# Indirect scatters on GpSimd tied to other engines' progress: the first sorting scatters after the twentieth follow VectorE, three of four result scatters per tile follow TensorE

## The chip, the cores and the metric

The kernel runs on one core of one Trainium2 chip. The metric is the device time of one execution in microseconds (us). Before the change three runs took 594.9, 598.07 and 599.07 us, median 598.07.

## The reference

What is computed is one block on x of 32 sequences of 256 tokens, 128 wide (8192 tokens). A layer norm is followed by two branches that are added to x: a gated linear recurrence ("the mixer": projection, causal convolution with 4 taps, a scan along the sequence, gates, output projection), and a mixture of 8 experts of which each token uses 2. Cut to what matters:

```python
x = L0_attn_x
xn = _layernorm(x, axis=-1)
x = x + _L0_attn_ref(xn, ...) + _L0_ffn_ref(xn, ...)

# mixer, per token and channel
_, h = jax.lax.associative_scan(_linrec_combine, (alpha_c, gated), axis=1)
y = h * C_gate + D * x_conv
out = jnp.einsum('blh,...', y * jax.nn.silu(z), W_out)

# experts
logits = xt @ w_gate
top_logits, sel = jax.lax.top_k(logits, TOP_K)          # TOP_K = 2
probs = jax.nn.softmax(top_logits, axis=-1)
h = silu(xt @ w1[e]) * (xt @ w3[e]);  y = h @ w2[e]
out = sum over the two chosen e of y * probs
```

## The kernel before, in words

The program is written by hand: each engine has its own list of instructions, and semaphores alone order them across engines. An instruction that is done adds one to its semaphore; a DMA adds 16 when it has landed. `wait_ge(s, n)` holds the engine's queue until semaphore s has reached n.

Stages:

- **Preparation.** x is loaded, normalised and transposed; TensorE makes the router's logits; VectorE chooses two experts for each token (`choose`) and counts a slot for each token and choice (`place(0)` for the first quarter of the tokens, `place(1)` for the rest). Then VectorE builds small tables (which expert each tile of sorted rows has, and where its rows begin): 38 short operations, most made with `link`, which adds one to `s_dve` and then waits for that same increment before it lets VectorE go on.
- **Sorting scatters.** GpSimd writes each token's normalised row to its two slots in a DRAM buffer `moe_in`: 64 groups of 128 tokens by 2 choices, so 128 indirect DMAs of 128 rows of 532 bytes, numbered i = 0 to 127 (line 540). The first 32 need `place(0)` alone. The function `ahead(i)` makes those from i = 49 on wait for `s_ch`, which counts VectorE's seven chain operations in each mixer step.
- **Mixer, steps 0 to 11.** Each step g takes 512 tokens. VectorE's part of a step is the convolution taps (`tap`, which counts `s_cv` after the second tap-pair of a kind and `s_taps` after the last), the chain of seven (`chain`, `s_ch`) and `softplus` (`s_dt`). Before these, ScalarE copies TensorE's projection out of PSUM, for which it waits on TensorE's `s_xr` and `s_xp`.
- **Experts.** 36 tiles of 512 sorted rows (the last has 256; four of them are split between two experts). SyncE loads each tile's rows and weights. TensorE's queue in one cycle is: first products of tile k (`up`: two halves, which count `s_h1` and `s_h3`), transposes of the rows of tile k + 1 (`transp`, `s_T`), second products of tile k - 1 (`down`, `s_y`). Between them ScalarE rounds (`xhi`, `whi`) and applies silu, and VectorE forms the low parts (`xlo`, `wlo`), the product of the halves (L1422) and the scaled result (`scale_y`, L1483, which counts `s_yc`) in a ring of 8 buffers. GpSimd then scatters the tile's result to `moe_out` in four indirect DMAs of 128 rows of 512 bytes (line 548): 142 in all. In the queue of before, all four of a tile wait only for `s_yc` and `s_dst` of that tile.
- **Mixer, steps 12 to 16, and the sums.** When all scatters have landed, GpSimd issues 16 accumulating DMAs (line 562) that add the experts' results; SyncE stores what is complete.

The order of the work is the order of each engine's list; no planner or scheduler is in it.

Of the kernel before, what the change touches and what calls it, by code (L numbers as in the profile page):

```python
# [22 lines left out]
EXPERTS, HID, TOP_K = 8, 256, 2  # L23
# [5 lines left out]
MOE_TILES = FULL + MIXED + 1  # L29
# [11 lines left out]
STEPS_A = 12  # L41
# [13 lines left out]
STORES = (5, 6)  # L55
OUTS = 8
CHAIN = 7


def block_kernel(nc, x, W_in, conv_w, conv_b, W_x, W_dt, b_dt, A_log, D_skip, W_out,  # L60
# [5 lines left out]
    with ctx:  # L66
# [6 lines left out]
        def sem(name):  # L73
            return ctx.enter_context(nc.semaphore(name))
# [140 lines left out]
        s_dve = sem("s_dve")  # L215
# [24 lines left out]
        s_taps = sem("s_taps")  # L240
        s_cv = sem("s_cv")
# [7 lines left out]
        s_dt = sem("s_dt")  # L249
# [3 lines left out]
        s_ch = sem("s_ch")  # L253
# [14 lines left out]
        s_T = sem("s_T")  # L268
        s_xhi = sem("s_xhi")
        s_xlo = sem("s_xlo")  # L270
        s_h1 = sem("s_h1")
        s_h3 = sem("s_h3")
# [39 lines left out]
                whole(g)  # L312


        def ahead(i):
            return min((i - 40) * 7 // 9 - 6, (STEPS_A - 2) * CHAIN)

        def logits_at(q):
            return (q + 1) % 2 * 512 + q // 2 * 256

        def rows_v(quarters):
            return sum(g < quarters * QT // GT for g in ROWS_V)

        def rows_a(quarters):
            return sum(g < quarters * QT // GT for g in ROWS_A)

        def rows_p(quarters):
            return sum(g < quarters * QT // GT for g in ROWS_P)
# [9 lines left out]
        def slots(t):  # L338
            return SUB if isinstance(t, int) and t == HALF else SLOTS
# [140 lines left out]
        def _(gp):  # L480
# [41 lines left out]
            for g in ROWS_P:  # L522
                normalise(g)
                if g == 6:
                    gp.wait_ge(s_wld, 16 * 10)
                    for k in range(TAPS):
                        gp.tensor_scalar(tap_raw[:, k, :], win_raw[:, 0, :], cw[:, 0, k:k + 1], None, ALU.mult).then_inc(s_tapw, 1)

            for n, (q0, qn) in enumerate(CHUNKS):
                gp.wait_ge(s_slot, n + 1)  # L530
                gp.wait_ge(s_xnp, rows_p(q0 + qn))
                if rows_v(q0 + qn):
                    gp.wait_ge(s_xn, rows_v(q0 + qn))
                if rows_a(q0 + qn):
                    gp.wait_ge(s_xna, rows_a(q0 + qn))
                for j in range(q0 * QT, (q0 + qn) * QT):
                    for k in range(TOP_K):
                        if ahead(j * TOP_K + k) > 0:
                            gp.wait_ge(s_ch, ahead(j * TOP_K + k))
                        gp.indirect_dma_start(xs_dram, bass.IndirectOffsetOnAxis(ap=slot_u[:, k, j:j + 1], axis=0),  # L540
                                              xn_row[:, j, :], None).then_inc(s_scat, 16)


            for t in range(MOE_TILES):
                gp.wait_ge(s_dst, t + 1)
                gp.wait_ge(s_yc, t + 1)
                for j in range(slots(t) // P):
                    gp.indirect_dma_start(yt_dram, bass.IndirectOffsetOnAxis(ap=dst_u[:, t, j:j + 1], axis=0),  # L548
                                          yo[t % OUTS][:, j, :], None, bounds_check=PAIRS - 1, oob_is_err=False).then_inc(s_ys[t % OUTS], 16)

# [316 lines left out]
        def _(act):  # L867
# [96 lines left out]
            def mix(g, slot, a, b, c, d, held=False):  # L964
                static = isinstance(g, int)
                nxt = (slot + 1) % SLOT3
                def conv():
# [6 lines left out]
                    if not (static and g < 2):  # L974
                        act.wait_ge(s_ch, g * CHAIN - CHAIN)
                    act.activation(xc[:, nxt, 0, 0:SEQ], PA[:, 0:SEQ], ACT.Silu, bias=cb[:, 0:1])
# [3 lines left out]
                def decay():  # L980
                    act.wait_ge(s_dt, g)
                    if not (static and g < 2):
                        act.wait_ge(s_ch, g * CHAIN - 2 * CHAIN + 1)
                    for c_ in range(HALVES):
# [4 lines left out]
                    if not (static and g < 2):  # L989
                        act.wait_ge(s_ch, g * CHAIN - 2 * CHAIN + 5)  # L990
                    act.activation(al[:, :, :], th[:, :, :], ACT.Copy, bias=0.5, scale=0.5).then_inc(s_al, 1)
# [122 lines left out]
        def _(ve):  # L1114
            count = [0]
# [97 lines left out]
            def chain(g, slot, part):  # L1213
# [8 lines left out]
                def after(n):  # L1222
                    ve.wait_ge(s_ch, g * CHAIN - CHAIN + n)
                if part == 0:
# [135 lines left out]
            place(1)  # L1360


            cnt = inc[:, TILES - 1, :]
            em = [P, EXPERTS, STEPS_T]
            link(ve.tensor_tensor(cmp_m, thr.unsqueeze(1).broadcast_to(em), cnt.unsqueeze(2).broadcast_to(em), ALU.is_lt))
# [169 lines left out]
            t = MOE_TILES - 1  # L1535
# [80 lines left out]
```

## Time and profile before

| what | us |
| --- | --- |
| median of three runs | 598.07 |
| profiled execution | 603.16 |
| its span on the core | 601.1 |
| TensorE busy | 466.7 (78%) |
| VectorE busy | 410.7 (68%) |
| ScalarE busy | 311.6 (52%) |
| GpSimd busy | 318.1 (53%) |
| sorting scatters, 128 | 141.2 |
| result scatters, 142 | 144.2 |

The profiled execution spends 2.1 us outside its span and is 5.1 us over the median of the other runs. PE is TensorE (PEld its weight loads), DVE VectorE, ACT ScalarE, POOL GpSimd, SP SyncE. Where the profile names who ended a wait, it goes by the record of the semaphore's increment. If the increment is recorded within 1.5 us of the end of the instruction that makes it, that instruction is named; if it came later than that, the wait is put down to "remote" or "another core or an unknown queue". This program runs on one core and has no remote partner.

### The profile page before, as it was taken

The numbers are of one execution on the slowest core, as the hardware profiler recorded it, in microseconds if no ns is written. First come the engines' busy times: TensorE is split into PE (matmuls) and PEld (weight loads), VectorE is DVE, ScalarE is ACT, GpSimd is POOL, SyncE is SP. The second block draws the span as 40 slices with busy tenths as digits, with TensorE's granted clock in tenths as the row PEclk, the third lists the DMA queues.
The fourth block names the chain that finished last, engine by engine and source line by source line (L and its number), as shares of the span: only waits on it lengthen the run. The fifth ranks groups of instructions, "written<-read, shape, count | busy, mean of one in ns | idle before, by whom it ended". The sixth has DMA issues, their size and how long they took to land.

```text
span 601.1 us, 8269 instructions
## 1 busy us (share of the span) xinstructions
PE 466.7 (78%) x2188; PEld 335.9 (56%) x2188; DVE 410.7 (68%) x868; ACT 311.6 (52%) x421; POOL 318.1 (53%) x345
## 2 busy tenths in 40 slices
PE   1994450688999999988976976877886798899864
PEld 1883220355555555555865765766765687765434
DVE  6997410499999999896854454454653564479996
ACT  3851110988888886977332332332332242359880
POOL 4657775077777767300655645647465556374310
PEclk9997695699999999989989988979898998699995
DMA  9301112611221212033555544434454454108993
GB/s 253 92 25 54 54 50 77 109 42 52 64 76 45 76 41 81 24 89 85 159 158 155 155 128 130 126 114 137 129 150 122 133 150 119 43 12 148 210 201 105
DMA packets 70939, 62.75 MB, mean 104 GB/s; under 512 B 9034, under 2 KB 63214, under 8 KB 70912
## 3 DMA queue, kind: packets, MB, share of 16 engines
q1 hardware_dynamic: 57728, 35.37, 22.0%
q0 software_dynamic: 10944, 25.52, 15.7%
q10 hardware_dynamic: 2240, 1.57, 0.9%
q8 instruction: 9, 0.15, 0.1%
q14 instruction: 18, 0.15, 0.1%
HBM read 38.94 MB, written 29.64 MB: 114 GB/s over the span
## 4 chain that ended last, share of the span: by engine, by line
PE 33%; another core or an unknown queue 18%; DVE 17%; issue 12%; ACT 9%; SPq 7%; DMA 3%; ACTq 0%; DVEq 0%
PE PD L813 6%; PE PC L661 4%; PE PD L634 3%; PE PB L648 3%; SPq L371 3%; DVE hbuf L1242 2%; DVE acc L1283 2%; DVE gbuf L1131 2%; PE PA L673 2%; PE PB L679 2%; PE PA L775 2%; DMA xnT<-in_L_ffn_w_dram 2%; DVE hbuf L1247 1%; PE PA L779 1%
## 5 line engine op out<-in xcount | busy, mean ns | idle before, releaser
L548 POOL DMA_INDIRECT moe_out<-xnT,dst_u x142 | 144.2, 1015 | 150.0 <-DVE xnT L1483 108.3
L540 POOL DMA_INDIRECT moe_in<-xn,slot_u x128 | 141.2, 1103 | 71.5 <-issue 41.5
L1422 DVE TENSOR_TENSOR xn<-xn,PB 128x1024 f32<-128x1024 f32 (+1 forms) x36 | 43.4, 1204 | 66.8 <-remote 36.2
L1068 ACT ACTIVATE xn<-PA 128x1024 f32<-128x1024 f32 (+1 forms) x36 | 36.5, 1014 | 70.4 <-remote 31.2
L1283 DVE SCALAR_TENSOR_TENSOR acc<-PA,cw,acc 128x255 f32<-128x255 f32 (+2 forms) x96 | 54.2, 607 | 25.7 <-ACT acc L977 22.6
L813 PE MATMUL PD<-xnT,xn 128*128 128x128 f32 x536 | 66.1, 276 | 1.1 <-DVE xnT L1483 1.0
L813 PEld LDWEIGHTS PD<-xnT,xn 128*128 128x128 f32 x536 | 63.1, 193 | 1.8 <-DVE xnT L1483 1.3
L661 PE MATMUL PC<-xc,Wc 128*128 128x512 f32 x128 | 58.2, 597 | 2.4 <-ACT xc L1024 2.4
L634 PE MATMUL PD<-xc,WgB 128*128 128x512 f32 x128 | 57.5, 592 | 0.0
L775 PE MATMUL PA<-xhi,whi 128*128 128x512 f32 x62 | 29.9, 482 | 34.6 <-ACT xhi L1062 21.3
L1062 ACT ACTIVATE xhi<-PD 128x512 fp32r<-128x512 f32 (+1 forms) x36 | 21.2, 590 | 56.8 <-remote 31.9
L1483 DVE TENSOR_TENSOR xnT<-PD,slot_p 128x512 f32<-128x512 f32 (+1 forms) x36 | 24.5, 681 | 33.1 <-remote 15.6
L648 PE MATMUL PB<-WoT,y 128*128 128x128 f32 x240 | 33.3, 297 | 16.4 <-DVE y L1259 11.4
L648 PEld LDWEIGHTS PB<-WoT,y 128*128 128x128 f32 x240 | 30.8, 207 | 22.1 <-DVE y L1259 13.8
L1036 ACT ACTIVATE whi<-xnT 128x512 fp32r<-128x512 f32 x36 | 22.6, 629 | 38.9 <-DMA xnT<-in_L_ffn_w_dram 33.3
L634 PEld LDWEIGHTS PD<-xc,WgB 128*128 128x128 f32 x128 | 24.2, 190 | 30.1 <-issue 30.1
L679 PE MATMUL PB<-xnT,WinT 128*128 (+1 forms) x64 | 31.9, 623 | 11.0 <-ACT dsk L886 11.0
L661 PEld LDWEIGHTS PC<-xc,Wc 128*128 128x128 f32 x128 | 23.6, 193 | 26.5 <-issue 23.2
L670 PE MATMUL PA<-xnT,WinT 128*128 (+1 forms) x32 | 17.4, 626 | 26.7 <-DVE acc L1283 26.7
L1242 DVE TENSOR_TENSOR_SCAN hbuf<-al,gbuf 128x512 f32<-128x512 f32 x32 | 37.3, 1207 | 0.1
L775 PEld LDWEIGHTS PA<-xhi,whi 128*128 128x128 f32 x62 | 13.0, 209 | 38.1 <-issue 35.6
L673 PE MATMUL PA<-xnT,Wtap 128*128 (+4 forms) x128 | 31.5, 391 | 0.0
(211 smaller groups left out, 990.7 us busy)
## 6 DMA issues: line engine op xcount, KB each, us to landing
xnT<-in_L_ffn_w_dram SPq DMA_DIRECT2D x108, 128.0 KB
xn<-moe_in SPq DMA_DIRECT2D x31, 266.0 KB
out_dram<-moe_out POOLq DMA_DIRECT2D x10, 512.0 KB, 10.4
out_dram<-xacc SPq DMA_DIRECT2D x7, 512.0 KB, 4.0
xacc<-moe_out POOLq DMA_DIRECT2D x6, 512.0 KB, 10.1
moe_out<-xnT,dst_u POOLq DMA_INDIRECT x142
moe_in<-zrow SPq DMA_DIRECT2D x8, 266.0 KB
moe_in<-xn,slot_u POOLq DMA_INDIRECT x128
```

The source lines that it names most:

```text
L540: gp.indirect_dma_start(xs_dram, bass.IndirectOffsetOnAxis(ap=slot_u[:, k, j:j + 1], axis=0), xn_row[:, j, :], None).then_inc(s_scat, 16)
L548: gp.indirect_dma_start(yt_dram, bass.IndirectOffsetOnAxis(ap=dst_u[:, t, j:j + 1], axis=0), yo[t % OUTS][:, j, :], None, bounds_check=PAI ...
L634: last = pe.matmul(PD[:, n * GROUP:(n + 1) * GROUP], WgB[:, n * 2 + k, :], xc[:, slot, k, :], start=(k == 0), stop=(k == 1))
L648: last = pe.matmul(PB[:, j * D:(j + 1) * D], y2[:, k, j * P:(j + 1) * P], WoT[:, k, :], start=(k == 0), stop=(k == 1))
L661: last = pe.matmul(PC[:, c_ * GROUP:(c_ + 1) * GROUP], Wc[:, k, c_ * P:(c_ + 1) * P], xc[:, slot, k, :], start=(k == 0), stop=(k == 1))
L673: last = pe.matmul(PA[:, j:SEQ], Wtap[:, TAPS - 1 - j, :], source(g, 0, SEQ - j), start=(j == 0), stop=(j == TAPS - 1))
L679: last = pe.matmul(PB[:, c_ * GROUP:(c_ + 1) * GROUP], WinT[:, INNER + c_ * P:INNER + (c_ + 1) * P], source(g), start=True, stop=True)
L775: pe.matmul(o, whi[:, b, at], xhi[:, b, :], start=True, stop=False)
L813: last = pe.matmul(PD[:, 512 + j * D:512 + (j + 1) * D], hid[b][:, k * SLOTS + j * P:k * SLOTS + (j + 1) * P], (w2x[t - FULL] if mixed and ...
L1242: last = ve.tensor_tensor_scan(hbuf[:, c_, :], al[:, c_, :], gbuf[:, c_, :], 0.0, ALU.mult, ALU.add)
L1283: ins = ve.scalar_tensor_tensor(a_v, p_v[:, :, 0:SEQ - j], cw[:, c_, TAPS - 1 - j:TAPS - j], a_v, ALU.mult, ALU.add)
L1422: ve.tensor_tensor(halves(hid[b], t), halves(sil, t), halves(PB[:, :], t), ALU.mult).then_inc(s_hid, 1)
```

## The change

It has two parts, both in GpSimd's list, and both add waits only; no instruction is added, removed or moved against another on any engine. Part one replaces `ahead(i)`: sorting scatters 21 to 31 wait for `s_dve`, two links further for each; 32 to 38 wait for points of mixer steps 0 and 1 (`s_cv`, `s_taps`, `s_dt`); 39 to 127 wait for `s_ch`. Part two makes the second, third and fourth result scatter of tile t wait for `s_h1` and `s_h3` of tile t + 2 and `s_T` of tile t + 3.

```diff
+TABLES_AT = 78
...
-        def ahead(i):
-            return min((i - 40) * 7 // 9 - 6, (STEPS_A - 2) * CHAIN)
...
+            def follow(i):
+                if 21 <= i < 32:
+                    gp.wait_ge(s_dve, TABLES_AT - 2 + 2 * (i - 21))
+                elif 32 <= i < 34:
+                    gp.wait_ge(s_cv, 3)
+                elif i == 34:
+                    gp.wait_ge(s_cv, 4)
+                elif i == 35:
+                    gp.wait_ge(s_taps, 2)
+                elif 36 <= i < 38:
+                    gp.wait_ge(s_dt, 1)
+                elif i == 38:
+                    gp.wait_ge(s_cv, 5)
+                elif i >= 39:
+                    gp.wait_ge(s_ch, min(1 + (i - 39) * CHAIN // 9, (STEPS_A - 2) * CHAIN))
...
-                        if ahead(j * TOP_K + k) > 0:
-                            gp.wait_ge(s_ch, ahead(j * TOP_K + k))
+                        follow(j * TOP_K + k)
...
                 for j in range(slots(t) // P):
+                    if j == 1:
+                        gp.wait_ge(s_h1, min(t + 3, MOE_TILES))
+                    elif j == 2:
+                        gp.wait_ge(s_h3, min(t + 3, MOE_TILES))
+                    elif j == 3:
+                        gp.wait_ge(s_T, min(t + 4, MOE_TILES))
```

GpSimd's list at the sorting scatters, before. `slot_u` holds the slots, `xn` the normalised rows; `x31` means 31 more of the same with no wait.

```order
L540 DMA moe_in<-xn,slot_u 69632x133 [waits s_xna,s_xnp,s_slot]
L540 DMA moe_in<-xn,slot_u 69632x133 x31
L540 DMA moe_in<-xn,slot_u 69632x133 [waits s_xn,s_xna,s_xnp,s_slot]
L540 DMA moe_in<-xn,slot_u 69632x133 x16
L540 DMA moe_in<-xn,slot_u 69632x133 [waits s_ch] x79
```

And now (the line is 553 in the changed file):

```order
L553 DMA moe_in<-xn,slot_u 69632x133 [waits s_xna,s_xnp,s_slot]
L553 DMA moe_in<-xn,slot_u 69632x133 x20
L553 DMA moe_in<-xn,slot_u 69632x133 [waits s_dve] x11
L553 DMA moe_in<-xn,slot_u 69632x133 [waits s_xna,s_xn,s_cv,s_xnp,s_slot]
L553 DMA moe_in<-xn,slot_u 69632x133 [waits s_cv] x2
L553 DMA moe_in<-xn,slot_u 69632x133 [waits s_taps]
L553 DMA moe_in<-xn,slot_u 69632x133 [waits s_dt] x2
L553 DMA moe_in<-xn,slot_u 69632x133 [waits s_cv]
L553 DMA moe_in<-xn,slot_u 69632x133 [waits s_ch] x89
```

Before, 49 scatters could go out with no wait between them; now 21 can, and of the rest 89 instead of 79 are spread over the mixer's chain steps.

GpSimd's list at the last two tiles of the experts and the first sums, before. `yo`, the ring of results, is part of `xnT`; `dst_u` holds the rows' homes.

```order
L548 DMA moe_out<-xnT,dst_u 16384x128 [waits s_yc,s_dst]
L548 DMA moe_out<-xnT,dst_u 16384x128 x3
L548 DMA moe_out<-xnT,dst_u 16384x128 [waits s_yc,s_dst]
L548 DMA moe_out<-xnT,dst_u 16384x128
L562 DMA xacc<-moe_out 128x1024 [waits s_ys_5,s_ys_4,s_ys_6,s_ys_3,s_ys_7,s_ys_2,s_base,s_ys_1,s_ys_0]
```

And now:

```order
L567 DMA moe_out<-xnT,dst_u 16384x128 [waits s_yc,s_dst]
L567 DMA moe_out<-xnT,dst_u 16384x128 [waits s_h1]
L567 DMA moe_out<-xnT,dst_u 16384x128 [waits s_h3]
L567 DMA moe_out<-xnT,dst_u 16384x128 [waits s_T]
L567 DMA moe_out<-xnT,dst_u 16384x128 [waits s_yc,s_dst]
L567 DMA moe_out<-xnT,dst_u 16384x128 [waits s_h1]
L581 DMA xacc<-moe_out 128x1024 [waits s_ys_5,s_ys_4,s_ys_6,s_ys_3,s_ys_7,s_ys_2,s_base,s_ys_1,s_ys_0]
```

The scatters stand in the same order; each now has a wait of its own, and the sums still wait for all of them.

## Rows read from the trace of the kernel before

**Rows 1.** Busy time by stage, all engines; first line names the columns.

```profile
core 0: us, PE busy (x) PEld busy (x) DVE busy (x) ACT busy (x) POOL busy (x), PEclk, DMA share, GB/s
62.70:92.30 29.60, 15.38 (x36) 7.32 (x36) 8.20 (x32) 3.77 (x8) 22.60 (x24) 0.79 0.16 53
92.30:107.00 14.70, 0.00 (x0) 0.00 (x0) 0.01 (x1) 0.93 (x2) 6.14 (x7) 0.50 0.22 70
107.00:118.80 11.80, 8.23 (x18) 5.20 (x19) 5.92 (x10) 11.54 (x14) 0.00 (x0) 0.61 0.80 139
118.80:266.20 147.40, 136.05 (x477) 78.19 (x476) 141.27 (x192) 127.73 (x152) 92.33 (x79) 0.99 0.19 60
284.50:530.50 246.00, 199.43 (x1161) 170.49 (x1160) 129.24 (x289) 78.95 (x109) 136.05 (x135) 0.91 0.45 131
```

**Rows 2.** Timeline, VectorE, 40 to 93 us: start, duration, what, [idle before, releaser].

```profile
40.90 0.42 DVE L1162 TENSOR_TENSOR y<-hbuf,gbuf 128x256 f32<-128x256 f32 x1
...
88.52 0.35 DVE L1396 TENSOR_SCALAR al<-al 128x40 f32<-128x40 f32 x1 [1.22 <-DVE src_i L1395]
...
92.03 0.18 DVE L1399 CAST eid_i<-al 128x40 int32<-128x40 f32 x1 [0.54 <-DVE pad_i L1398]
```

**Rows 3.** Timeline, all engines, 64 to 108 us.

```profile
64.59 0.96 POOL L540 DMA_INDIRECT moe_in<-xn,slot_u  x1 [0.31 <-issue]
...
73.21 1.88 PE L673 MATMUL PA<-xnT,Wtap 128*128 128x256 f32 x8
...
99.31 0.96 POOL L540 DMA_INDIRECT moe_in<-xn,slot_u  x1 [0.30 <-issue]
106.07 0.47 ACT L976 ACTIVATE xc<-PA,cb 128x256 f32<-128x256 f32 x1 [22.37 <-remote]
...
107.03 3.48 DVE L1283 SCALAR_TENSOR_TENSOR acc<-PA,cw,acc 128x255 f32<-128x255 f32 x6 [14.73 <-ACT acc L977]
```

**Rows 4.** Timeline, GpSimd and ScalarE in the mixer, 226 to 241 us.

```profile
226.02 1.17 POOL L540 DMA_INDIRECT moe_in<-xn,slot_u  x1 [3.15 <-issue]
...
240.18 1.27 ACT L1006 ACTIVATE ebuf<-PC,bdt 128x512 f32<-128x512 f32 x2 [3.44 <-remote]
```

**Rows 5.** Waits, 300 to 520 us: us in total, times, longest.

```profile
DVE xn L1422 <- remote: 36.2, 7, 6.3
...
ACT xhi L1062 <- remote: 31.9, 9, 6.5
```

**Rows 6.** Timeline of three cycles of the experts, 356 to 373 us.

```profile
356.82 0.47 PE L775 MATMUL PA<-xhi,whi 128*128 128x512 f32 x1
...
359.91 0.98 POOL L548 DMA_INDIRECT moe_out<-xnT,dst_u  x1 [2.40 <-DVE xnT L1483]
...
361.81 0.47 PE L775 MATMUL PA<-xhi,whi 128*128 128x512 f32 x1
...
362.81 0.62 PE L779 MATMUL PA<-xlo,whi 128*128 128x512 f32 x2
...
365.07 0.98 POOL L548 DMA_INDIRECT moe_out<-xnT,dst_u  x1 [0.30 <-issue]
...
367.07 1.02 ACT L1068 ACTIVATE xn<-PA 128x1024 f32<-128x1024 f32 x1 [3.11 <-remote]
...
371.32 1.22 DVE L1422 TENSOR_TENSOR xn<-xn,PB 128x1024 f32<-128x1024 f32 x1 [6.23 <-remote]
...
372.21 0.79 PE L775 MATMUL PA<-xhi,whi 128*128 128x512 f32 x1 [4.68 <-ACT xhi L1062]
```

**Rows 7.** Result scatters, all: duration in ns, smallest, median, largest.

```profile
L548 POOL DMA_INDIRECT moe_out<-xnT,dst_u x142: 982/985/1806, 288.6 to 539.7; - x142
```

**Rows 8.** Timeline: first loads of sorted rows, last scatter, last sum.

```profile
258.81 0.94 SPq L447 DMA_DIRECT2D xn<-moe_in  x2
...
539.65 0.98 POOL L548 DMA_INDIRECT moe_out<-xnT,dst_u  x1 [0.30 <-issue]
...
576.30 0.89 POOL L562 DMA_DIRECT2D xacc<-moe_out  x1 [1.64 <-DMA xacc<-moe_out]
```

More of the change, by code:

```diff
@@ L1360, in _ @@
             place(1)
+            assert count[0] == TABLES_AT
             cnt = inc[:, TILES - 1, :]
```

## The prediction

> **What bounds the kernel now.** I read the busy times by stage first, then the timeline where every engine is idle at once, then the waits of the experts' stage, then the timeline of a few expert cycles.
>
> By stage: from 118.8 to 266.2 us the mixer runs with VectorE busy 141.3 of 147.4 us, so VectorE bounds it, and GpSimd's 79 scatters there cost little [rows 1]. Two other stretches have no busy engine at their head. From 62.7 to 92.3 us VectorE is busy 8.2 of 29.6 us, and from 92.3 to 107.0 us nobody computes (TensorE 0.00, VectorE 0.01, ScalarE 0.93 us) [rows 1]. In the experts' stage, 246.0 us for 35 intervals between the second products of 36 tiles, TensorE is busy 199 us at a clock of 0.91, with the others below it [rows 1]: 7.03 us a tile.
>
> What the engines wait for is their own semaphores. While the tables are built a short VectorE operation waits 1.22 us for the increment of the one before it; at 40.9 us, with the scatters only just begun, the same kind of link shows no idle time [rows 2]. TensorE ended its convolution at 75.1 us, and ScalarE, which needs nothing else, took it up at 106.07 us, 31 us later; VectorE's taps follow at 107.03 us [rows 3]. All this time GpSimd issues scatters back to back, 0.96 us with 0.30 us between them, to 100.3 us [rows 3]. So the increments are late, and they are late when scatters run without a pause. Two more places say the same. In the mixer the scatters run at 79 in 147.4 us, one per 1.87 us, and nothing is late, except after a 3.15 us hiccup of GpSimd at 226 us that it then makes up without pausing: ScalarE gets TensorE's increment 3.44 us late [rows 4]. In the experts' stage a cycle takes 4.99 us when nothing is late (356.82 to 361.81), and 10.4 us (361.81 to 372.21) when eight scatters follow one another from 359.91 us on; the first product ended at 363.4 us and ScalarE saw it at 367.07 us, VectorE its half at 371.32 us [rows 6]. Such late increments ("remote") are counted nine times at ScalarE's rounding between 300 and 520 us [rows 5].
>
> Why eight follow one another: a scatter takes 0.985 us and 0.30 us to the next, so four take 5.14 us, more than the 4.99 us of an undisturbed cycle [rows 6, 7]. GpSimd falls behind, never pauses, and after about two cycles everything stalls until it runs out of work.
>
> **The change, part by part.** No instruction is added or removed, so nothing but waits and their effects counts.
>
> *Scatters 0 to 20* are as before; number 21, the first with a new wait, began at 64.59 us [rows 3], so the late increments up to there stay.
>
> *Scatters 21 to 31.* Their waits ask for two links each. The first five are granted by then. From about 70 us on the tables lag: with late increments a link takes some 1.4 us (1.22 idle and about 0.2 of work), two take 2.8 us, more than a scatter's 1.26, so GpSimd pauses and the increments catch up. The tables then need their own busy time, 8.2 us, plus little between. From 62.7 us that alone ends at 71 us; the first seven to eight microseconds of it are still disturbed, so I take 78 us where 92.2 us was [rows 1, 2]. GpSimd stops at scatter 31, before the taps of step 0, rather than at 48; 11 scatters at 1.26 us from 64.6 us also end at 78.5 us. TensorE's convolution, over at 75.1 us, is then seen at about 80.5 us and the taps begin at 82 to 83 us, against 107.03 us. **Gain 24 us.** Bounds: if the increments come the moment TensorE ends, taps start at 77 us, gain 30. If all eleven must first go out at the disturbed pace of 2.8 us (from 65 to 96 us), gain 11.
>
> *Scatters 32 to 38* lie beside steps 0 and 1, where VectorE, ScalarE and TensorE take 11.8 us to the first chain step and GpSimd was idle [rows 1]. Seven scatters there, at least one event apart, cost nothing; were they to disturb it, by the one case in the mixer, 3.4 us [rows 4].
>
> *Scatters 39 to 127* keep the pattern of nine per seven chain steps, begun ten scatters earlier in number but at the same chain step. The last waits for chain step 69 instead of 61, about 13 us later against the mixer. Queued behind it is nothing but the result scatters; waiting for it is SyncE, which loads the first sorted rows. It issued those at 258.81 us, held by other waits, while TensorE's second products begin at 284.5 us [rows 1, 8]. A last landing at about 262 us of the old time scale leaves some ten microseconds. Cost nothing; were that cover gone, the lateness itself, up to 5 us.
>
> *Result scatters.* Where nothing is late, the new waits are already granted: the result of tile t is scaled in the middle of the first products of tile t + 2, and the second scatter comes 1.29 us later, so a wait binds only when an increment is over about 2.7 us late. Then it stops GpSimd within a scatter or two instead of after eight. In the long cycle of [rows 6]: the first scatter of the next tile goes at 365.07 us, the second now waits for the increment of 363.4 us, GpSimd is idle from 366.05 us, the increments arrive by about 367, ScalarE rounds by 368 and TensorE starts at about 368.5 us, not 372.21. That is 6.7 us for 10.4, **3.7 us** a long cycle. I count 10 or 11 of these in the stage, nine in the 220 us of [rows 5]: 38 to 41 us. **Gain 38 us.** Bounds: GpSimd's own pace, 142 times 1.285 = 182.5 us, is the least the stage can take, a gain of 63. The other end is 0 if the short stalls are as many as the waits they save, and below that the fourth rival.
>
> *The end.* The sums need all scatters. The last began at 539.65 us, the last sum is issued at 576.30 us, and the core ends at 601.1 us [rows 8]. GpSimd may be a little further behind TensorE than now: nothing to 4 us, taken as nothing.
>
> Sum: 603.2 - 24 - 38 = 541 us for the profiled execution. It stands 5.1 us over the median of 598.07, so in the timed runs **536 us**.
>
> *A rule against it.* ScalarE and TensorE are late in the stretch 92.3 to 107.0 us, in which VectorE was busy 0.01 us [rows 1]. The Trainium skill (SBUF — State Buffer, "Who interferes with whom") says that only the port pair shared by VectorE and GpSimd causes contention and that PE and ACT never wait on anyone. By that rule the scatters could harm VectorE's operations alone, spacing them would give back nothing of these waits, and the sum would be the time of before. The trace disagrees: the waits are on ScalarE and TensorE too.
>
> **Rivals.**
>
> 1. *Only the first part works* (12 in 100). At the experts' undisturbed pace the new waits are granted in advance, and GpSimd still needs 5.14 us for a cycle of 4.99. If the first scatter of each tile, which has no new wait, and the three granted ones suffice to choke the increments, long cycles stay as they are. Against it: in the long cycle the increment needed was over 3 us late. 598 - 24 = 574 us.
> 2. *Only the second part works* (6). What is queued after 28 scatters drains no faster, as after 100.3 us, when the first increments still took 5.8 us. 598 - 38 = 560 us.
> 3. *The waits have another cause than the unbroken scatters* (6), such as a port lock between VectorE and GpSimd. GpSimd's scatters in the experts' stage would only be moved by a microsecond or two beside the same VectorE operations. 598 us. This is the rule of the Trainium skill named above.
> 4. *GpSimd becomes the bound* (7). At 5.14 us a cycle it has no time to spare, so each idle moment at a new wait is lost for good. If each of three waits costs 1 us, the delay seen in a disturbed link, a tile takes 8.2 us, the ring of eight results fills, VectorE waits for it, and the stage takes 35 times 8.2 = 287 us, 41 more; with the first part's 24 that is 598 + 17 = 615 us. It decides from a mean of 7.7 us a tile on. Against it: a pause lets the increments catch up, and then the waits are granted.
> 5. *Everything is cleared* (4): 598 - 28 - 63 = 507 us.
>
> **How the numbers follow.** The forecast has 65 in 100, with 515 to 560 us of its own. Rivals 1, 2 and 5 are faster too: 87 in 100. A measurement of this kernel tells about 1% from no change, here 6 us: same 6 in 100, slower 7. The range goes from 510 us (gains of 28 and 60) to 576 us (11 and 11, which takes in the first and second rival): it leaves out rivals 3 to 5 and a little of the forecast's tails.
>
> **What would show it.** Right: VectorE's tile table (the last of the short operations) ends near 78 us and the first step's taps start before 88 us; the expert cycle's mean falls from 7.03 to below 6.2 us with none of 9 us or more; GpSimd's waits in that stage name TensorE's first products. The mixer's ten steps stay at 147 us together, so that the whole gain lies in these two stretches. Wrong: late increments remain in cycles of 10 us (rival 1), taps after 100 us (2), VectorE waiting for the ring (4). The forecast fails above all if increments are late not for want of pauses but for another traffic that the waits leave as it is.

## The result and the profile after

The changed kernel takes 560.43 us (median of four runs, 554.35 to 569.29) beside 597.03 us for the kernel before (four runs, 594.9 to 599.07), 37 us less. The ratio is **0.931, interval 0.9235 to 0.9384**. Ratios here and below are of fast runs alone, without those over 1.5% above the fastest of their kernel (here 563.62 and 569.29 us), so this one stands for a mean of 555.8 us, 41 us less. The forecast was 536 us with a range of 510 to 576: the direction and the range hold, and of the 62 us forecast 37 to 41 came. The profiled execution took 557.25 us (before 603.16), with a span of 555.1 us (601.1): 46 us less. It is the second fastest of the four, and that of before was the slowest of its kernel, so the traces overstate the gain between the medians by some 9 us.

The same stages as in [rows 1], in the changed kernel (columns as there):

```profile
62.70:79.70 17.00, 9.88 (x23) 5.27 (x24) 9.23 (x37) 5.93 (x11) 9.83 (x10) 0.66 0.12 40
79.70:94.35 14.65, 14.65 (x40) 7.41 (x39) 5.93 (x11) 10.26 (x13) 8.02 (x9) 1.00 0.59 147
94.35:240.26 145.91, 133.17 (x473) 76.25 (x472) 141.06 (x191) 128.39 (x152) 106.18 (x90) 1.00 0.23 67
256.50:483.00 226.50, 190.88 (x1160) 162.49 (x1158) 127.39 (x288) 78.24 (x109) 138.75 (x136) 0.95 0.50 142
483.00:555.10 72.10, 56.37 (x204) 35.27 (x204) 63.90 (x85) 46.19 (x55) 19.96 (x22) 0.88 0.69 139
```

Stage by stage against [rows 1]:

| stretch | before | changed | less by |
| --- | --- | --- | --- |
| start to the taps of step 0 | 107.0 | 79.7 | 27.3 |
| taps of step 0 to the first chain step | 11.8 | 14.65 | -2.85 |
| ten mixer steps | 147.4 | 145.9 | 1.5 |
| to the second products of the experts' first tile | 18.3 | 16.2 | 2.1 |
| 35 expert intervals | 246.0 | 226.5 | 19.5 |
| the rest | 70.6 | 72.1 | -1.5 |

They add up to the 46 us. The idle 14.7 us in which nobody computed is gone, and TensorE's granted clock in the experts' stage is 0.95 where it was 0.91.

**The tables.** VectorE's short operations and GpSimd's scatters in the changed kernel, timeline (start, duration, what, [idle before, releaser]), 66 to 80 us. VectorE:

```profile
71.00 0.18 DVE L1394 SCALAR_TENSOR_TENSOR al<-al 128x16 f32<-128x16 f32 x1 [1.92 <-remote]
...
73.12 0.19 DVE L1398 TENSOR_TENSOR xc<-xc,al 128x31 f32<-128x31 f32 x1 [1.74 <-remote]
...
79.61 0.41 DVE L1421 TENSOR_SCALAR tile_r<-al 128x40 f32<-128x40 f32 x1
79.70 1.13 DVE L1302 SCALAR_TENSOR_TENSOR acc<-PA,cw,acc 128x255 f32<-128x255 f32 x2
```

GpSimd and ScalarE in the same stretch:

```profile
68.12 0.96 POOL L553 DMA_INDIRECT moe_in<-xn,slot_u  x1 [0.31 <-issue]
71.24 0.96 POOL L553 DMA_INDIRECT moe_in<-xn,slot_u  x1 [2.16 <-remote]
74.08 1.41 POOL L553 DMA_INDIRECT moe_in<-xn,slot_u  x1 [1.88 <-DVE xc L1399]
76.53 0.96 POOL L553 DMA_INDIRECT moe_in<-xn,slot_u  x1 [1.03 <-DVE y L1405]
```

```profile
68.90 0.60 ACT L903 ACTIVATE Wc<-PB 128x512 f32<-128x512 f32 x1 [13.86 <-remote]
...
76.98 0.47 ACT L995 ACTIVATE xc<-PA,cb 128x256 f32<-128x256 f32 x1 [1.37 <-PE PA L692]
```

GpSimd stops for 2.16 and 1.88 us at the new waits, and behind the second stop the links have lost their idle time: the table ends at 79.7 us, not 92.2. TensorE's convolution ends at 76.94 us and ScalarE takes it up at 76.98; in the kernel before the same instruction (L976 there) started at 106.07 us, 31 us after that end [rows 3]. The first late wait of ScalarE, 13.86 us, is none of this: it ended at 68.90 us, just before GpSimd's first stop at 69.08, and before the change the same wait was 12.5 us and ended at 67.53.

**Steps 0 and 1.** GpSimd and ScalarE, 84 to 95 us:

```profile
89.20 0.96 POOL L553 DMA_INDIRECT moe_in<-xn,slot_u  x1 [0.30 <-issue]
94.65 1.77 POOL L553 DMA_INDIRECT moe_in<-xn,slot_u  x1 [4.49 <-DVE acc L1302]
```

```profile
92.17 0.47 ACT L995 ACTIVATE xc<-PA,cb 128x256 f32<-128x256 f32 x1 [3.43 <-remote]
```

From 77.79 to 89.20 us ten scatters (28 to 37) go out without a pause, although the last six have the new waits on `s_cv`, `s_taps` and `s_dt`: these were granted at once. Only number 38 waits, to 94.65 us. And increments are late again: TensorE's convolution of step 1 ends at 88.5 us and ScalarE takes it up at 92.17.

**The experts.** Waits of the changed kernel, 256 to 485 us (us in total, times, longest); they answer to [rows 5]:

```profile
ACT xhi L1081 <- remote: 28.1, 8, 5.0
...
POOL moe_out L567 <- PE PA L798: 24.3, 5, 21.3
DVE xnT L1503 <- remote: 24.1, 10, 3.6
DVE xn L1442 <- remote: 23.1, 8, 3.9
...
POOL moe_out L567 <- remote: 15.3, 10, 1.9
...
POOL moe_out L567 <- PE PD L776: 4.2, 4, 2.0
```

GpSimd now waits for TensorE's first products and transposes (the 21.3 us is the start of the stage), and ten times for an increment that is itself late. But ScalarE and VectorE still wait for late increments. The longest of them are shorter at ScalarE's rounding (5.0 us for 6.5) and VectorE's product (3.9 for 6.3), while VectorE's scaled result waits ten times for 24.1 us where it was eight times for 15.6. The scatters themselves are as before [rows 7]:

```profile
L567 POOL DMA_INDIRECT moe_out<-xnT,dst_u x142: 982/985/1787, 260.6 to 490.4; - x142
```

One cycle that stayed long, in which TensorE's second products are at 272.36 and at 282.82 us:

```profile
271.24 1.18 POOL L567 DMA_INDIRECT moe_out<-xnT,dst_u  x1 [0.30 <-issue]
...
272.72 0.98 POOL L567 DMA_INDIRECT moe_out<-xnT,dst_u  x1 [0.30 <-issue]
...
274.01 0.98 POOL L567 DMA_INDIRECT moe_out<-xnT,dst_u  x1 [0.30 <-issue]
...
274.44 1.22 DVE L1442 TENSOR_TENSOR xn<-xn,PB 128x1024 f32<-128x1024 f32 x1 [2.88 <-remote]
275.30 0.98 POOL L567 DMA_INDIRECT moe_out<-xnT,dst_u  x1 [0.30 <-issue]
...
277.27 0.60 ACT L1081 ACTIVATE xhi<-PD 128x512 fp32r<-128x512 f32 x1 [4.02 <-remote]
...
277.97 0.47 PE L794 MATMUL PA<-xhi,whi 128*128 128x512 f32 x1 [3.66 <-issue]
278.01 0.98 POOL L567 DMA_INDIRECT moe_out<-xnT,dst_u  x1 [1.73 <-remote]
```

TensorE's transposes were over at 272.5 us and ScalarE saw them at 277.27. Three scatters go out after that end, the last of a run of eleven without a pause from 260.57 us on; then GpSimd is held, for 1.73 us, to 278.01.

### The profile page after: what moved, and what is told of

It reads as the page before. It is cut to its first block, busy times and chain, and to the rows that moved or that the text cites. A ratio compares the mean times of both kernels' runs of the same rounds, so it can differ in the third digit from the quotient of the medians.

```text
span 555.1 us, 8269 instructions
## 1 busy us (share of the span) xinstructions
PE 454.9 (82%) x2188; PEld 326.3 (59%) x2188; DVE 410.1 (74%) x868; ACT 311.0 (56%) x421; POOL 321.4 (58%) x345
## 4 chain that ended last, share of the span: by engine, by line
PE 34%; DVE 22%; issue 15%; another core or an unknown queue 11%; SPq 7%; ACT 6%; DMA 3%; DVEq 0%; ACTq 0%
PE PC L680 5%; PE PD L653 4%; PE PB L667 4%; PE PD L832 4%; DVE hbuf L1261 3%; DVE acc L1302 3%; PE PB L698 3%; SPq L369 3%; PE PA L692 2%; DVE gbuf L1150 2%; DVE hbuf L1266 2%; DVE hbuf L1272 1%; PE PA L689 1%; DVE y L1278 1%
## 5 line engine op out<-in xcount | busy, mean ns | idle before, releaser
L553 POOL DMA_INDIRECT moe_in<-xn,slot_u x128 | 144.1, 1126 | 61.4 <-issue 37.6
L1081 ACT ACTIVATE xhi<-PD 128x512 fp32r<-128x512 f32 (+1 forms) x36 | 21.2, 589 | 48.0 <-remote 28.1
L1503 DVE TENSOR_TENSOR xnT<-PD,slot_p 128x512 f32<-128x512 f32 (+1 forms) x36 | 24.5, 681 | 28.2 <-remote 24.1
L794 PE MATMUL PA<-xhi,whi 128*128 128x512 f32 x62 | 27.6, 444 | 20.2 <-issue 12.0
L698 PE MATMUL PB<-xnT,WinT 128*128 (+1 forms) x64 | 32.0, 624 | 12.5 <-ACT dsk L905 12.5
L1448 DVE TENSOR_TENSOR wlo<-xnT,whi 128x512 fp32r<-128x512 f32 x36 | 24.9, 691 | 11.4 <-ACT whi L1055 7.0
L1435 DVE TENSOR_TENSOR xlo<-PD,xhi 128x512 fp32r<-128x512 f32 (+1 forms) x36 | 24.5, 679 | 10.2 <-ACT xhi L1081 6.9
L776 PE MATMUL PD<-ident,xn 128*128 128x128 f32 x142 | 22.5, 281 | 10.8 <-DMA xn<-moe_in 9.1
## 6 DMA issues: line engine op xcount, KB each, us to landing
out_dram<-moe_out POOLq DMA_DIRECT2D x10, 512.0 KB, 10.1
```

Source lines behind the costliest of these rows:

```text
L698: last = pe.matmul(PB[:, c_ * GROUP:(c_ + 1) * GROUP], WinT[:, INNER + c_ * P:INNER + (c_ + 1) * P], source(g), start=True, stop=True)
L794: pe.matmul(o, whi[:, b, at], xhi[:, b, :], start=True, stop=False)
```

## The experiments

Twelve runs were made, of seven kernels, on three chips. Which chip the measurement above, the first one, ran on is not on record. The short edits, all against the kernel before or the changed one:

First part alone (the changed kernel without the waits in the scatter loop of the experts):

```diff
                 for j in range(slots(t) // P):
-                    if j == 1:
-                        gp.wait_ge(s_h1, min(t + 3, MOE_TILES))
-                    elif j == 2:
-                        gp.wait_ge(s_h3, min(t + 3, MOE_TILES))
-                    elif j == 3:
-                        gp.wait_ge(s_T, min(t + 4, MOE_TILES))
```

> Only the first part of the change: sorting scatters from number 21 on follow VectorE; the result scatters wait as before. Theory (late increments come from scatters without a pause, in two separate stretches): the taps of step 0 start near 80 us, the experts' stage starts 25 to 28 us earlier and then lasts as long as before, 246 us; ratio to before 0.95 to 0.96. Rival (the parts act on each other, since GpSimd enters the experts' stage later than before): the experts' stage changes by over 8 us with no edit in it.

Second part alone: the kernel before with those six lines.

> Only the second part: the second to fourth result scatter of a tile wait for TensorE's points; the sorting scatters wait as before. Theory: the stretch to the first chain step stays at 118.8 us, the experts' stage falls from 246 to about 226 us as in the changed kernel; ratio 0.96 to 0.97. Rival (the waits are granted in advance and the shorter stage of the changed kernel is luck of one execution): stage 240 us or more, ratio 0.99 to 1.00.

No result scatters. The sum of the experts is left out, zeros are written in its place by one DMA behind the stage (its lines, and those of the zeros' buffer and semaphores, are left out of both cuts below):

```diff
-                for j in range(slots(t) // P):
-                    gp.indirect_dma_start(yt_dram, ...).then_inc(s_ys[t % OUTS], 16)
+                gp.sem_inc(s_ys[t % OUTS], 16 * (slots(t) // P))
```

> Before, with the 142 result scatters left out (GpSimd adds their 16 increments at once; zeros are written to the buffer after the stage, so the experts' sum is missing from the output). Theory: no late increments, every cycle of the experts 5.0 to 5.5 us, second products from first to last tile in 180 to 195 us instead of 246. Rival (the weight loads or TensorE's clock make the long cycles): 230 us or more.

Each result scatter replaced by a multiplication on GpSimd at the same place, with no DMA (again the sum of the experts is left out):

```diff
-                    gp.indirect_dma_start(yt_dram, ...).then_inc(s_ys[t % OUTS], 16)
+                    gp.wait_ge(s_scr, 4 * t + j + 1)
+                    gp.tensor_scalar(scr[:, :], scr[:, :], 1.0, None, ALU.mult).then_inc(s_scr, 1)
+                gp.sem_inc(s_ys[t % OUTS], 16 * (slots(t) // P))
```

> Before, with each result scatter replaced by one GpSimd multiplication of a 128x512 scratch tile in place (about 1 us, reads and writes SBUF, one increment); output without the experts' sum. Theory (it is the scatters' own traffic that holds the increments): as without scatters, 180 to 195 us for the stage, no wait put down to remote. Rival (a port shared by VectorE and GpSimd, or GpSimd being busy at all): VectorE's operations get longer or the cycles stay at 6 us or more, 215 us or more.

These four ran on one chip, and there the kernel before took 491.79 us, not 597:

| kernel | us | before beside it | ratio, interval |
| --- | --- | --- | --- |
| first part alone | 491.73 | 491.79 | 0.9995, 0.9976 to 1.0013 |
| second part alone | 491.80 | 491.79 | 0.9987, 0.9968 to 1.0007 |
| no result scatters (one run) | 500.40 | 491.79 | |
| multiplications (one run) | 560.50 | 491.79 | |

These runs decide between no theory and its rival, since what both take for given was missing: **no increment is late in the traces of this chip**. (The 181.2 us of the stage with multiplications lie in the theory's range, but by GpSimd's own pace; the second part's ratio is the rival's, with nothing to gain.) Between 60 and 540 us the waits put down to "remote" are 42 with 174.8 us in the first measurement's trace of before, 50 with 139.6 us in that of the change, and none in those of the first and of the second part alone here. The experts' stage of the first part alone, whose result scatters are those of the kernel before, and of the kernel with no result scatters:

```profile
239.20:413.10 173.90, 173.22 (x1161) 155.64 (x1160) 129.92 (x289) 80.11 (x109) 130.60 (x129) 1.00 0.64 184
```

```profile
239.80:413.10 173.30, 172.76 (x1161) 155.82 (x1160) 129.37 (x288) 80.22 (x109) 0.00 (x0) 1.00 0.51 137
```

With 129 scatters the stage takes 173.9 us, with none 173.3. TensorE is busy throughout at full clock. So the scatters as such cost 0.6 us at most, one trace against one, and the 72 us more that the kernel before takes in this stage in the first measurement go with late increments, the lower clock (0.91) included. That the kernel without scatters takes 500.40 us in all goes with the DMA of the zeros, for which GpSimd waits 23.9 us before the sums. Does GpSimd pause there? The first part alone, GpSimd from 300 us on, and TensorE's second products beside it:

```profile
300.16 0.98 POOL L561 DMA_INDIRECT moe_out<-xnT,dst_u  x1 [0.30 <-issue]
...
301.45 0.98 POOL L561 DMA_INDIRECT moe_out<-xnT,dst_u  x1 [0.30 <-issue]
...
302.74 0.98 POOL L561 DMA_INDIRECT moe_out<-xnT,dst_u  x1 [0.31 <-DVE xnT L1497]
...
304.02 0.98 POOL L561 DMA_INDIRECT moe_out<-xnT,dst_u  x1 [0.30 <-issue]
```

```profile
299.87 1.95 PE L826 MATMUL PD<-xnT,xn 128*128 128x128 f32 x16
...
304.84 1.95 PE L826 MATMUL PD<-xnT,xn 128*128 128x128 f32 x16
```

It doesn't: the same 1.29 us from one scatter to the next as in [rows 6], and a cycle of 4.97 us beside it. Nor do the sorting scatters disturb: in the second part alone, where the first 49 go out back to back as before, the taps of step 0 start at 67.48 us. **Unbroken scatters are not enough to make an increment late.** The multiplications take 1.49 us each (median of 142) where a scatter takes 0.985:

```profile
301.33 6.57 POOL L553 TENSOR_SCALAR scr<-scr 128x512 f32<-128x512 f32 x4 [0.18 <-POOL scr L553]
308.08 6.33 POOL L553 TENSOR_SCALAR scr<-scr 128x512 f32<-128x512 f32 x4 [0.18 <-DVE dst_u L1475]
```

That is 6.4 to 6.8 us a tile for a cycle of 5: GpSimd falls back without end, the ring of eight is full from about tile 30 on (cycles of 5.4 to 6.5 us from there), and GpSimd catching up to 476.8 us and the DMA of the zeros make up the rest of the 560.5 us. Up to there, two cycles at the start apart, TensorE's cycle is 5.0 us with GpSimd never idle. It shows that a GpSimd busy in SBUF doesn't slow the others here; for a chip with late increments it says nothing.

**Does the effect come back elsewhere?** The kernel before and the change, unaltered, on another chip than that of the four runs: the second measurement.

> The kernel before, unchanged, once more. In the last four runs no increment was late on that chip, in kernels with and without the scatters' new waits, and before took 491.8 us there, not 597. Theory A (late increments belong to the chip or its surroundings, not to the program): a run is either at 490 to 495 us with all cycles of the experts at 5.0 us, or near 597 us with the long cycles of the first trace. Theory B (they vary from execution to execution on one chip): times between.

> The changed kernel on the same chip. Where increments are late: ratio 0.92 to 0.95 as first measured. Where they are not: GpSimd's new waits in the experts are granted in advance and the result is 0.998 to 1.003, no difference.

There the kernel before takes 608.22 us (seven runs, 605.41 to 619.08; the one profiled took 613.49) and the change 574.28 (four runs, 573.5 to 575.63): **0.9438, interval 0.9356 to 0.952**. The experts' stage of before and of the change on this chip, and between them the change's stretch from taps to chain:

```profile
289.80:537.00 247.20, 196.17 (x1161) 167.11 (x1159) 127.21 (x288) 77.59 (x108) 137.34 (x136) 0.92 0.45 130
```

```profile
77.85:94.93 17.08, 16.75 (x45) 8.02 (x43) 5.93 (x11) 10.25 (x13) 9.58 (x10) 1.00 0.40 126
267.30:500.20 232.90, 190.45 (x1160) 160.99 (x1158) 127.46 (x288) 77.62 (x110) 137.43 (x136) 0.96 0.48 138
```

The taps start at 107.14 us before and 77.85 us changed, the first chain step at 118.80 and 94.93: 23.9 us in the first part's stretch, 14.3 us in the experts. Waits put down to "remote" are 50 with 205.0 us before and 54 with 158.2 us changed. The gains repeat in both stretches, but not the pauses. GpSimd is held once at the sorting scatters, at number 21:

```profile
68.35 0.96 POOL L553 DMA_INDIRECT moe_in<-xn,slot_u  x1 [4.45 <-DVE gbuf L1227]
```

Then 17 scatters, 21 to 37, go out without a pause to 90.3 us. All the same the links run without idle time to the taps at 77.85 us; late is only what comes behind many scatters in a row, TensorE's convolution of step 1, which ends at 86.0 us and is taken up at 92.75. As far as one trace can say, what counts is how many scatters have gone since the last pause, not that each has one of its own.

So late increments are not a property of the program alone. Whether they were seen on one chip or on two is open, since the first measurement may have run on this one.

The traces with late increments differ from the others in one thing more. Of the sorting scatters' landing increments, 16 for each of 128 or 2048 in all, the two traces of before hold 839 and 939, the two of the change 1005 and 1040; of the ten traces without late increments nine hold 2048 and one 2047. The semaphore did reach 2048 in each, for SyncE waits for that count before it loads sorted rows. It shows in the profile's lines of DMA issues, of the kernel before (first measurement) and of the first part alone, where the last number is the median time to landing in us:

```profile
moe_in<-xn,slot_u POOLq DMA_INDIRECT x128
```

```profile
moe_in<-xn,slot_u POOLq DMA_INDIRECT x128, 2.4
```

Whether the increments came merged or only their records are missing, the traces don't tell.

**Second and third attempt at the split.** The two parts alone and the multiplications again, with one kernel more: a GpSimd instruction between result scatters, to see whether a pause that waits for nobody does the same.

```diff
                 for j in range(slots(t) // P):
+                    gp.memset(scr[:, (4 * t + j) * 8:(4 * t + j + 1) * 8], 0.0)
                     gp.indirect_dma_start(yt_dram, ...)
```

> Only the first part of the change, once more, now hoping for a chip with late increments (before near 600 us; where it is at 492 us nothing can be told). Theory: the two parts are separate; the first chain step comes near 95 us instead of 118.8, the experts' stage stays at about 246 us, ratio 0.955 to 0.965. Rival (the first part gives the whole gain, the second none): ratio 0.93 to 0.945.

> Only the second part. Theory: first chain step at 118.8 us as before, the experts' stage 10 to 20 us shorter, ratio 0.97 to 0.985, and the two ratios multiply to that of the whole change. Rival: ratio 0.995 to 1.005.

> Each result scatter replaced by about 1 us of GpSimd arithmetic in SBUF, output without the experts' sum; zeros are written after the stage. Theory (the scatters' own traffic holds the increments): where before has long cycles this has none, 5.0 to 5.3 us each, second products over 180 to 190 us. Rival (GpSimd busy, or a port): long cycles of 9 us and more stay.

> Before, with a small GpSimd memset of 8 elements in front of each result scatter, so that they are 0.15 to 0.3 us further apart, about 1.5 us; no new wait. Theory (a pause of some tenths is enough for the increments to keep up, as at one per 1.59 us in the mixer): GpSimd's pace of 6.0 to 6.3 us a tile sets the cycle, no cycle over 9 us, stage 210 to 225 us. Rival (it is not the pause but the number of scatters in a row): bursts get longer and the stage is no shorter, 240 us or more.

They met the first experiments' chip again: first part 492.07 us beside 492.02 (1.0005, 0.999 to 1.002), second part 492.61 (1.0002, 0.9987 to 1.0018), multiplications 560.83, memset 491.77. One of the 19 runs of before took 577.12 us at a granted clock of 0.756, and one of the ten of the second part 656.59 us at 0.658. Neither has a trace, so whether increments were late in them isn't known. The memset tested nothing, and would not have on any chip:

```profile
299.21 0.98 POOL L550 DMA_INDIRECT moe_out<-xnT,dst_u  x1 [0.18 <-issue]
300.18 0.14 POOL L549 MEMSET scr<- 128x8 f32 x1
300.50 0.98 POOL L550 DMA_INDIRECT moe_out<-xnT,dst_u  x1 [0.18 <-issue]
```

Its 0.14 us fit into the gap that is there anyway; from scatter to scatter it is still 1.29 us.

> Only the first part of the change; worth reading if before is near 600 us here. Theory (separate parts): first chain step near 95 us, ratio 0.955 to 0.965 where the whole change gave 0.931 and 0.944, second products over 245 us or so as in both traces of before. Rival (the first part gives all): 0.93 to 0.945 and a shorter experts' stage.

> Each result scatter replaced by GpSimd arithmetic in SBUF (1.6 us each, as measured on the undisturbed chip); output without the experts' sum, zeros written after the stage. If before is near 600 us here. Theory (the scatters' own traffic holds the increments): the experts' cycles are 5.0 to 5.4 us up to tile 25 or so, then GpSimd's own pace of 6.5 us shows through the ring; 181 us from first to last second product. Rival (GpSimd busy is enough): cycles of 9 us and more stay.

This was a third chip, undisturbed too: first part 491.82 us beside 491.85 (0.9994, 0.9979 to 1.0009), multiplications 561.02. The first part's stages there, from the taps of step 0 to the first chain step and over the ten mixer steps, are the measure of what late increments cost:

```profile
67.40:79.35 11.95, 8.64 (x19) 5.24 (x20) 6.20 (x11) 4.35 (x7) 9.21 (x10) 0.71 0.98 175
79.35:221.50 142.15, 134.92 (x478) 77.24 (x477) 140.78 (x191) 126.71 (x151) 107.99 (x96) 1.00 0.25 72
```

## Why the prediction was right, and where it was wrong

**The tables (a gain of 24 us): right in sum, and by luck, since two errors cancel.** The links go slow until GpSimd is held, then run at their own pace, as forecast. The taps start at 79.70 us where 82 to 83 was forecast (before 107.03): 27.3 us. TensorE's convolution was seen at 76.98 us, as it ended, not 5 us later as was taken, and so no longer ended the wait; the tables did. But scatters 32 to 38, costed at nothing, follow 28 to 31 without a pause, and the first chain step comes 2.85 us later behind the taps than before (5.4 in the second measurement, 17.08 for 11.66). The 3.4 us that stood as their bound hold in the first and not in the second. The step "at least one event apart" failed: VectorE had run through the taps and the softplus of step 0 by 85.3 us, 5.6 us after it began, and the six scatters behind these points, at 1.26 us each from 82.87 us on, never found one that had not been passed. Net 24.5 and 23.9 us.

**Mixer, last sorting scatters, the end: right.** 145.9 us for 147.4; the first sorted rows are issued at 241.34 us, and what TensorE's transposes of them wait for at 247.68 us is ScalarE's last work in the mixer:

```profile
247.68 0.66 PE L776 MATMUL PD<-ident,xn 128*128 128x128 f32 x4 [1.11 <-ACT thg L1039]
```

The last scatter ends 8.4 us after the last tile's second products begin (10.1 before), and the end is 1.5 us longer, within the 0 to 4.

**Result scatters (a gain of 38 us): the term that failed, by half.** It measured 19.5 us, and 14.3 in the second measurement. "Below 6.2 us with none of 9 us or more" is 6.47 us, with four of 9 us or more. From the starts of the tiles' second products, what the 35 cycles have above 5 us:

| | in cycles of 9 us or more | in all others | together |
| --- | --- | --- | --- |
| before | 61.4 (10 cycles) | 9.6 | 71.0 |
| changed | 21.7 (4) | 29.8 | 51.5 |
| before, second measurement | 52.1 (7) | 20.1 | 72.2 |
| changed, second measurement | 19.7 (4) | 38.2 | 57.9 |

The long cycles gave back 39.7 us, about the forecast 38, and the short ones took 20.2 of it again (32.4 and 18.1 in the second measurement). Two sentences of the working failed. The first is that the wait "stops GpSimd within a scatter or two": in the cycle shown above three pass after the end that ScalarE waits for, and eight had gone before them without a pause. The trace shows why. The first scatter of each tile has no new wait, and the others ask for points of TensorE that a scatter reaches only when their increments are already some us late; until then they are granted. The second is that "the increments arrive by about 367", that is, that a pause of a microsecond clears everything: pauses of 1 to 2 us now stand where one of 2.4 us stood [rows 6], and each clears a part. This reading is from the trace alone; no run with other points tested it.

**Rival 3 and the rule.** The first part's and the second part's stretches both got shorter where only GpSimd's issue times changed, in both measurements, so some cause that the spacing leaves as it is can't be all of it. ScalarE still waits for late increments (28.1 us in eight), as in the cycle above, where TensorE had long been done. The Trainium skill (SBUF — State Buffer, "Who interferes with whom") says that PE and ACT never wait on anyone, but of contention for ports of SBUF. Of that the undisturbed chips agree: TensorE is busy 173.22 of 173.9 us beside scatters, 172.76 of 173.3 without. The prediction took the sentence to be about semaphores too; it doesn't cover the late increment.

**Rivals 1, 2, 4 and 5.** Both stretches gained, so neither part alone is the whole (1, 2) as far as two traces without the parts apart can say. GpSimd's loss at the new waits never filled the ring (4): GpSimd still waited 13 times, 24.7 us in all, for VectorE's next scaled result, and so had caught up. Rival 5's price for everything cleared, 507 us, was 15 us above what a chip without late increments shows (and takes 28 us for the tables where the working has 30).

**The sum.** 62 us were taken off one profiled execution. The trace gave 46; the medians 37 and 34. The prediction carried the whole gain over from an execution 5 us above its median; part of the late increments that it counted may be of that execution alone, which no second trace of before from that measurement shows.

**What stays open.** What makes an increment late. The prediction's cause, scatters without a pause, is at most half of it: breaking their row helps where increments are late, and unbroken ones do no harm on two other chips. No run tells whether the difference lies in the chips, in what else ran beside them, in the moment or in the memory that the buffers got. The two parts alone never met late increments; that the first is worth 24 us and the second 14 to 20 rests on stages of the traces. Not run either: four waits per tile, nearer points, and no scatter in steps 0 and 1, which by the numbers above is worth some 3 to 5 us.

## What to carry to other kernels

A wait that is to space out transfers must fall on a point that is passed no faster than the transfers go; count the interval between those points against the issue time, not their number, and don't leave the first of each group free. (That such points would have given the rest of the forecast is argued, not run.) Before costing a stall that shows as an increment recorded long after its instruction ended, find out whether it belongs to the program: the same kernel run again, at other times and on other chips, said more here (597, 608, 492 us) than any edit. A gain read from a single disturbed execution is an upper estimate; what vanishes from its long stalls comes back partly in short ones.

## What the runs showed of the chip that was not expected

- The kernel before takes 595 to 599 us in one measurement, 605 to 619 in another and 492 us (median) on two other chips. Against the first part alone, undisturbed, its trace is longer where waits for late increments stand: the start up to the taps takes 107.0 and 67.4 us, the ten mixer steps 147.4 and 142.15, the experts' stage 246.0 and 173.9. Behind the experts it is 5 us shorter (70.6 and 75.7).
- The traces with late increments hold 839 to 1040 of the sorting scatters' 2048 landing increments, all others 2047 or 2048.
- On an undisturbed chip 142 scatters of 128 rows beside TensorE's bound stage cost it 0.6 us of 173.9 at most, at a DMA share of 0.64 where without them it is 0.51.
- TensorE's clock follows the stalls: granted 0.91 and 0.92 in the experts' stage with late increments before the change, 0.95 and 0.96 after it, 1.00 where none is late and the engine never stands still.
- A GpSimd multiplication of 128x512 takes 1.49 us, and its memset of 128x8 0.14 us, which fits unseen into the 0.30 us between two scatters.
